# Routed rows of the experts: the exponential goes behind the GELUs and the token copy, the top-two work behind the splits

## The reference

```python
def _L0_ffn_ref(hidden, router_w, router_b, sw1, sb1, sw2, sb2, rw1, rb1, rw2, rb2):
    flat = hidden.reshape(T, d)                      # T = 8 * 512 tokens, d = 256
    router_probs = softmax(flat @ router_w + router_b)      # 8 experts
    topk_probs, topk_idx = jax.lax.top_k(router_probs, 2)
    weights = zeros_like(router_probs).at[arange(T)[:, None], topk_idx].add(topk_probs)
    shared_out = gelu(flat @ sw1 + sb1) @ sw2 + sb2
    h1 = gelu(einsum('td,edh->teh', flat, rw1) + rb1[None])
    expert_out = einsum('teh,ehd->ted', h1, rw2) + rb2[None]
    return shared_out + einsum('ted,te->td', expert_out, weights)
```

## Time and profile before

| | |
|---|---|
| median of 3 runs | 4081.86 us (4077.23 to 4085.93) |
| the profiled execution, its own time | 4082.73 us |
| its span, first to last instruction | 4080.9 us |
| mean granted TensorE clock | 0.949 of full speed |
| busy: PE, DVE, ACT, POOL | 3623.4, 2915.8, 1929.7, 1633.9 us |
| routed sequences of moe_a, moe_b | 562.99 to 691.53 us, 1857.65 to 1987.55 us |

### The profile page before, as it was taken

The page is one execution under the profiler, slowest core; times in us unless marked ns, Lnnn a source line. Parts: engine busy times, 40 slices in busy tenths (PEclk is TensorE's granted clock), DMA queues, the critical chain, the costliest instruction groups (busy, mean ns, idle before and its releaser), DMA issues. The chain is left out here.

```text
span 4080.9 us, 60197 instructions
## 1 busy us (share of the span) xinstructions
PE 3623.4 (89%) x19256; PEld 2605.9 (64%) x19256; DVE 2915.8 (71%) x5355; ACT 1929.7 (47%) x4079; POOL 1633.9 (40%) x1485
## 2 busy tenths in 40 slices
PE   4888878999599999998799788987999899999998
PEld 3455557889488888887789634544666455554666
DVE  5777657676566666645677578886888676766998
ACT  3565644444455555544344344442444466656332
POOL 3776726454566666633555411101003445441000
PEclk8999979999899999998899889989999899999999
DMA  5999902565100000001266400002102444441000
GB/s 136 303 256 275 304 32 73 167 202 170 48 19 17 19 19 19 19 2 38 95 186 195 154 24 17 19 11 43 21 0 49 91 111 101 103 110 25 11 15 16
DMA packets 228874, 358.33 MB, mean 88 GB/s; under 512 B 36482, under 2 KB 132851, under 8 KB 221811
## 3 DMA queue, kind: packets, MB, share of 16 engines
q1 hardware_dynamic: 204038, 265.38, 22.4%
q0 software_dynamic: 24544, 89.36, 9.0%
HBM read 173.82 MB, written 172.20 MB: 85 GB/s over the span
## 5 line engine op out<-in xcount | busy, mean ns | idle before, releaser
L2895 DVE TENSOR_REDUCE ab_nmx<-banks 128x1 f32<-128x512 f32 x512 | 329.3, 684 | 136.6 <-PE banks L2682 134.2
L2826 ACT ACTIVATE ab_pt<-banks 128x512 f32<-128x512 f32 x512 | 283.2, 600 | 162.0 <-PE banks L2692 152.9
L1737 POOL TENSOR_TENSOR lb_pq<-lb_pq,lb_rr 128x512 f32<-128x512 f32 x192 | 206.2, 1077 | 305.1 <-DVE lb_rr L1598 301.7
L1463 ACT ACTIVATE lb_pq<-banks,lb_nmx 128x256 f32<-128x256 f32 x384 | 178.5, 470 | 230.0 <-DVE lb_nmx L1593 226.8
L2692 PE MATMUL banks<-ab_qT,ab_kT 128*128 128x512 f32 x512 | 253.2, 500 | 5.3 <-ACT ab_pt L2826 5.3
L358 ACT ACTIVATE da_pt<-banks 128x512 f32<-128x512 f32 (+1 forms) x384 | 179.1, 537 | 123.4 <-PE banks L270 119.1
L1593 DVE TENSOR_REDUCE lb_nmx<-banks 128x2 f32<-128x512 f32 x192 | 131.1, 683 | 146.5 <-PE banks L1315 145.2
L2682 PE MATMUL banks<-ab_kT,ab_qT 128*128 128x512 f32 x512 | 209.1, 411 | 18.5 <-DVE ab_nmx L2895 13.7
L285 PE MATMUL banks<-da_pt,da_vx 128*64 128x512 f32 (+3 forms) x1024 | 166.3, 470 | 34.4 <-POOL da_pt L578 30.8
L576 POOL TENSOR_TENSOR da_pt<-da_pt,w_da_tri 128x384 f32<-128x384 f32 x128 | 150.4, 1175 | 87.0 <-ACT da_pt L358 86.9
L2466 PE MATMUL banks<-w_f_dT,f_hT 128*128 128x256 f32 x768 | 178.3, 382 | 4.0 <-ACT f_hT L2512 4.0
(11 more groups left out here) (538 smaller groups left out, 11180.4 us busy)
## 6 DMA issues: line engine op xcount, KB each, us to landing
moe_xs<-zero SPq DMA_DIRECT2D x71, 512.0 KB, 11.5
moe_ys<-zero SPq DMA_DIRECT2D x71, 512.0 KB, 11.5
moe_a_w_raw<-in_moe_w SPq DMA_DIRECT2D x48, 512.0 KB, 3.9
moe_b_w_raw<-in_moe_w SPq DMA_DIRECT2D x48, 512.0 KB, 3.8
da_spill<-da_hi SPq DMA_DIRECT2D x128, 128.0 KB, 2.4
ab_spill<-ab_hi SPq DMA_DIRECT2D x128, 128.0 KB, 2.4
ab_qT<-ab_spill POOLq DMA_DIRECT2D x32, 392.0 KB, 5.8
ab_kT<-ab_spill POOLq DMA_DIRECT2D x32, 392.0 KB, 5.5
```

Of the source, the lines that this page charges most:

```text
L1463: nc.scalar.activation(pq[:, n % RING, t, :], ps[:, S_BANK + n % 2, 2 * P * t:2 * P * t + 2 * P], ACT.Exp, bias=nmx[:, n % RING, t:t + 1], ...
L1737: nc.gpsimd.tensor_tensor(pq[:, n % RING, :, :], pq[:, n % RING, :, :], bcast(rr[:, n % RING, :], 2, 2 * P), ALU.mult).then_inc(s_p, 1)
L2826: nc.scalar.activation(pt[:, s % RING, :], ps[:, EXP_BANK + s % 3, :], ACT.Exp, scale=AB_D ** -0.5).then_inc(s_e, 1)
L2895: nc.vector.tensor_reduce(nmx[:, g % 2, col:col + 1], ps[:, MAX_BANK + n % 3, :], op=ALU.max, axis=AX.X, negate=True).then_inc(s_mx, 1)
```

## The change

On ACT the exponential of sequence i+1 moves from ahead of the GELUs of i+1 to behind these and the token copy of i+2. On DVE `weights(i+1)` moves from behind the first split of i+1 to behind all four splits and `low_x(i+2)`, still ahead of `take(i)`. No instruction is added or taken away.

```diff
@@ scalar
                 for i in range(-3, N):
-                    if i + 1 in routed:
-                        exponentials(routed[i + 1])
                     if i + 1 in number:
                         hidden(i + 1)
                     if i + 2 in turned:
                         copy_tokens(i + 2)
+                    if i + 1 in routed:
+                        exponentials(routed[i + 1])
                     if i + 2 in load_of and loads[load_of[i + 2]][1] == i + 2:
                         high_w1(load_of[i + 2])
@@ vector
                     if i + 1 in routed:
                         logits(routed[i + 1])
                     if i + 1 in number:
-                        split_hidden(i + 1, 0)
-                    if i + 1 in routed:
-                        weights(routed[i + 1])
-                    if i + 1 in number:
-                        for m in range(1, HCH):
+                        for m in range(HCH):
                             split_hidden(i + 1, m)
                     if i + 2 in number:
                         low_x(i + 2)
+                    if i + 1 in routed:
+                        weights(routed[i + 1])
                     if i in number:
                         take(i)
```

## The result

The changed kernel takes 4111.72 us (median of 4 runs, 4109.75 to 4115.12) against 4083.89 us of the kernel before in the same comparison: ratio 1.0079, 95% interval 1.0063 to 1.0096. It is slower: the two medians differ by 28 us, and the recorded ratio, which is not the quotient of these medians, stands for 32 us (26 to 39). Forecast was 4117 from 4082, 35 us. The profiled execution's span went from 4080.9 to 4108.0 us.

The account below looks back on a forecast made before the run. The bound was taken to be a loop of waits across PE, ACT, DVE and POOL in the routed steps, not PE itself. Per stage 4.9 + 8.5 + 0 + 4.0 = 17.4 us, twice +35: 4081.9 to 4117 us, range 4096 to 4134.

Parts of the forecast that it names:

- The exponential moves at no cost: ACT: the exponential, now behind the token copy, is ready before DVE asks for it; table loads stay the same in number.
- `weights` behind `low_x` puts copy, high part, low part, `weights`, `ranks` and `logits` in series with `up`: Middle steps: `ranks` waits for `weights`, now behind the low part; PE pauses 2.2 us ahead of `ranks`.
- The series is 17.3 us at the upper clock: Sum of the new loop from one `up` to the next: 17.3 us against 17.65 before, a gain of 0.35.
- The clock costs 2.1 us a step: PE's clock falls around the pause and light routing matmuls, slowing `logits` and `up`: 2.1 us a step, ends 0 and 3.9.
- the rival in which it holds: PE's clock stays at its upper level: terms 3.3 + 0.2 + 3.1 = 6.6 us a stage, 4095 us; chance 0.12.
- First step +4.9: Item 0 to 1: `ranks` waits 9.05 us behind the transposition, so `up` starts at 591.95 instead of 587.05.
- Items 5 to 7: 0: Item 6 has no `up`, `weights(5)` no low part ahead; `turn_tokens(7)` comes about as before, 0.
- Last step +4.0: Item 7: `weights` stands behind `low_x(8)`, so `ranks(7)` comes 3.6 us later, up to 1 more; taken as +4.0.
- Nothing takes the lateness up: Behind `ranks(7)` all is in series to the first unit's load, so the lateness reaches the end whole.
- The range: 4096 to 4134 us, said to hold the forecast and nearly all of the clock-holds and clock-stays-low rivals; 2 in 10 outside.
- The gain of the stall: PE's wait for GELUs in `up`, up to 2.28 us, goes because GELUs no longer wait for the exponential.
- The rival of the faster loop: Loop closes over PE's own work: 15.05 us a step, 9 us less a stage, 4076 with the ends; chance 0.03.

Follow-up runs that it names:

- filled run: Changed kernel plus 8 matmuls of 448 columns on PE, results unused, ahead of `ranks` of sequences 1 to 6 in each stage; ratio 1.0051 to before.
- run of VectorE's half: Changed kernel with the exponential back ahead of the GELUs, `weights` still behind `low_x`; 4106.79 us, ratio 1.0068 to the kernel before.

## Why the prediction was right

The direction, the place and the time were right: 4111.72 us lies between 4096 and 4134, 5 us under the forecast; as a difference it is 28 or 32 us, by medians or by ratio, against 35. Part of the closeness is luck: the four steps and items 5 to 7 together came out 3 and 2 us shorter than forecast in the two stages, while the first steps were 1.6 and 0.4 us longer. Step by step:

- *The exponential moves at no cost.* Right. It was ready 0.73 us before its use, and putting it back changed nothing that the intervals tell. The number of table loads did not stay, as the prediction says, but fell by one a stage, which nothing waited for.
- *`weights` behind `low_x` puts copy, high part, low part, `weights`, `ranks` and `logits` in series with `up`.* Right, shown from both sides: `weights` ahead of `low_x` takes most of the loss away, `weights` behind `take` adds to it.
- *The series is 17.3 us at the upper clock.* 16.9 was measured in the two steps of the filled run at that clock. `up` took 5.55 us instead of 5.8, and from `logits` to the next `up` 1.8 instead of 2.0; the high part took 1.4 as forecast. In the change's own steps at the lower clock it took 1.04. At the upper clock the middle of the stage would even be a gain: 4 x 16.9 is 67.7 us against 69.1 and 69.3.
- *The clock costs 2.1 us a step.* That it falls in every step came true (0.84 to 0.87 in all eight), and the rival in which it holds fell. That 2.1 was measured too is partly luck: the number was picked between 1.8 and 3.9, not worked out, and the 2.5 us that PE lost were offset by 0.4 elsewhere in the chain. So the term was 6.4 and 7.4 instead of 8.5 and 8.3, nearly all of the difference by the series.
- *First step +4.9.* +6.5 and +5.3. `ranks` came 10.2 and 10.5 us behind the transposition, not 9.05, for one instruction of `weights` was held up by 2 us (last section), a term that the sum did not have. The rest of the way was 0.8 and 0.5 us shorter than the sum.
- *Items 5 to 7: 0.* They gained 0.9 and 0.8 us. The run with `weights` ahead of `low_x` gained 0.8 there too; why is not shown.
- *Last step +4.0.* +4.4 and +3.1.
- *Nothing takes the lateness up.* Right: from `ranks` of sequence 7 to the first unit the time is the same to 0.1 us, and POOL's scatters hid nothing.
- *The range.* It is said to hold nearly all of the rival in which the clock holds, but that rival's own 4095 lies just outside 4096 to 4134.
- *The gain of the stall.* The GELU waits of `up`, 6.2 us in moe_a, did go. They had been slack in a loop that was closed elsewhere: the transposition behind `up` ended at 612.31, and the copy that reads it could not start before 616.95. So that time was not on the path.

The rival of the faster loop, 15.05 us a step, did not come true in this kernel, but with `weights` ahead of the splits it did: 14.3 to 16.5 us.

## What to carry to other kernels

When work is moved back on one engine, look at what stands behind its consumer on the next engine: here PE's `ranks` stood ahead of the next `up`, so 4 us of small VectorE instructions joined the loop. Of the five places tried for `weights` the best was where its engine would in part be idle anyway, before the bulk work whose inputs are not there yet. A stall that disappears is a gain only if it lay on the loop that sets the step.

## What the runs showed of the hardware

The first step was longer than its sum because two instructions met, one on DVE and one on POOL (timelines of the changed kernel, moe_a):

```profile
584.65 2.17 DVE L977 TENSOR_TENSOR moe_a_logits<-moe_a_logits,moe_a_rs 128x32 f32<-128x32 f32 x1
```

```profile
584.43 2.34 POOL L1122 TENSOR_TENSOR moe_a_w_lo<-moe_a_w_raw,moe_a_w_hi 128x1024 fp32r<-128x1024 f32 x1 [1.46 <-ACT moe_a_w_hi L941]
```

The DVE instruction takes 0.19 us in the other sequences of moe_a; here it ends at 586.82, POOL's at 586.77. In moe_b it took 2.17 us again, beside POOL's 2.35. By the Trainium skill (SBUF — State Buffer, Who interferes with whom) VectorE and GpSimd share one pair of ports as an exclusive lock, which a VectorE instruction with two inputs in SBUF needs against a GpSimd instruction that reads SBUF, and the one that comes second blocks for the whole of the other; the trace agrees, 2.17 against 0.19 us.

The collision was there before the change, on another instruction, the low part:

```profile
583.63 3.37 DVE L1063 TENSOR_TENSOR moe_a_x_lo<-x_normed_T,moe_a_x_hi 128x1024 fp32r<-128x1024 f32 x1 [0.93 <-POOL moe_a_x_hi L1120]
```

It takes 1.23 us for items 2 to 5; here, for item 1, POOL's 2.35 us began 0.07 us ahead of it. In the run of VectorE's half it is the low part again, 3.35 us. So the row that would have warned of the missing 2 us stood in the trace of before, in the very step that the prediction summed.

TensorE's granted clock fell in the light matmuls behind a pause of 1.39 us, although 8 us of dense matmuls stood just ahead of that pause, and in another run behind light matmuls with PE idle for 0.1 us in 14.6. With six pauses of a stage filled six of the eight steps were still below 1.00, down to 0.85. The rule of idle gaps of the Trainium skill (TensorE: Matmul & The Clock Gate, HAM oscillation — how this bites in real kernels), weighed in the prediction, does not cover that.
